# A Mamba block and a mixture of experts on one core: a product moved from VectorE to GpSimd, the gate-up product one slot later, rank matmuls merged

## The reference

```python
x = x + mamba(layernorm(x))     # D_INNER 512, D_STATE 16, D_CONV 4
x = x + moe(layernorm(x))       # 8 experts, top 2, hidden 352, and a shared expert
# in mamba, over the tokens of a sequence:
dA = exp(clip(dt[:, :, None] * A, -5, 5))
state = dA * state + dt[:, :, None] * B[:, None, :] * u[:, :, None] + 1e-06
y = sum(state * C[:, None, :], axis=-1) + D * u
# in moe:
combine = top-2 softmax weights, 0 elsewhere          # tokens x experts
out = sum_e combine[e] * (silu(x @ wg[e]) * (x @ wu[e])) @ wd[e]
out = out + sigmoid(x @ sgw) * (silu(x @ sg) * (x @ su)) @ sd    # shared expert
```

## Time and profile before

| | us |
|---|---|
| median of 3 runs | 2950.19 (2948.59 to 2950.59) |
| the profiled execution, its own time | 2948.53 |
| its span, first to last instruction | 2946.7 |
| busy: PE / PEld / DVE / ACT / POOL | 2601.8 / 2291.2 / 2246.7 / 2030.5 / 2235.6 |
| mean granted TensorE clock | 0.923 of full |

### The profile page before, as it was taken

One profiled execution on the slowest core, in us unless ns is written; L12 is line 12 of the kernel. 1 busy time (PEld: TensorE's weight loads), 2 busy tenths in 40 slices (PEclk: granted clock), 3 DMA queues, 4 the chain that ended last, 5 costly groups with the idle time before them and its releaser, 6 DMA issues.

```text
span 2946.7 us, 49244 instructions
## 1 busy us (share of the span) xinstructions
PE 2601.8 (88%) x15616; PEld 2291.2 (78%) x15616; DVE 2246.7 (76%) x4890; ACT 2030.5 (69%) x4675; POOL 2235.6 (76%) x1354
## 2 busy tenths in 40 slices
PE   7888888888888888888888888888887599999998
PEld 4777877878787778877877778787776488888887
DVE  2989999999998999899989989998998233333332
ACT  3878888888888888888888888888875133333332
POOL 2989998989898989889998989898986033333333
PEclk9889999999999989999999999899987699999999
DMA  4222222222222222222222222222221288888886
GB/s 171 83 77 76 77 77 83 77 76 86 92 83 80 78 84 85 77 88 79 77 76 82 79 76 82 94 85 80 73 81 35 95 199 202 201 202 201 202 200 152
DMA packets 138184, 309.67 MB, mean 105 GB/s; under 512 B 15040, under 2 KB 79680, under 8 KB 137792
## 3 DMA queue, kind: packets, MB, share of 16 engines
q1 hardware_dynamic: 110848, 270.03, 29.5%
q0 software_dynamic: 27072, 36.46, 6.2%
HBM read 258.42 MB, written 48.01 MB: 104 GB/s over the span
## 4 chain that ended last, share of the span: by engine, by line
PE 52%; DVE 22%; ACT 10%; issue 8%; POOL 2%; DMA 1%; SPq 0%; DVEq 0%; ACTq 0%; POOLq 0%
PE bank L662 13%; DVE bank L1242 10%; PE bank L680 9%; PE bank L563 7%; PE bank L600 6%; DVE room L1242 4%; PE bank L552 4%; DVE room L1251 4%; ACT bank L809 3%; ACT room L793 3%; PE bank L530 2%; PE bank L580 2%; PE bank L616 2%; PE bank L570 2%; PE bank L644 2%
## 5 line engine op out<-in xcount | busy, mean ns | idle before, releaser
L1031 POOL TENSOR_TENSOR room<-dtu,b_all 128x1024 f32<-128x1024 f32 x512 | 1202.6, 2370 | 26.4 <-DVE dtu L1419 13.5
L809 ACT ACTIVATE bank<-room,eps_col 128x512 f32<-128x512 f32 x1024 | 693.9, 683 | 282.6 <-DVE carry L1256 202.4
L793 ACT ACTIVATE room<-room,neg_a 128x256 f32<-128x256 f32 x2048 | 867.9, 497 | 0.8 <-DVE room L1208 0.8
L600 PE MATMUL bank<-ident,room 128*128 128x128 f32 x4096 | 589.8, 295 | 236.8 <-DVE room L1251 215.7
L600 PEld LDWEIGHTS bank<-ident,room 128*128 128x128 f32 x4096 | 513.1, 153 | 302.1 <-DVE room L1251 232.3
L1020 POOL TENSOR_TENSOR room<-room,c_all 128x1024 f32<-128x1024 f32 x224 | 532.1, 2375 | 122.9 <-DVE bank L1242 87.7
L1242 DVE TENSOR_TENSOR_SCAN bank<-room,carry,bank 128x256 f32<-128x256 f32 x864 | 580.5, 735 | 48.6 <-ACT bank L809 47.7
L1156 POOL DMA_INDIRECT out<-room,ids x144 | 223.8, 1554 | 409.8 <-DMA out<-room,ids 217.9
L1321 DVE SCALAR_TENSOR_TENSOR hid<-hid,bank 128x256 f32<-128x256 f32 (+1 forms) x312 | 131.1, 420 | 453.8 <-ACT hid L904 453.7
L1242 DVE TENSOR_TENSOR_SCAN room<-room,carry,bank 128x256 f32<-128x256 f32 x672 | 446.1, 728 | 1.1 <-DVE hot L1292 0.5
L552 PE MATMUL bank<-xnT,w_conv 128*128 128x256 f32 x3072 | 404.2, 288 | 7.0 <-ACT xnT L832 5.5
(11 more groups left out here) (150 smaller groups left out, 3095.4 us busy)
## 6 DMA issues: line engine op xcount, KB each, us to landing
b_all<-b_scratch SPq DMA_DIRECT2D x128, 512.0 KB, 4.0
c_all<-b_scratch SPq DMA_DIRECT2D x128, 512.0 KB, 5.5
room<-in_wgu SPq DMA_DIRECT2D x72, 704.0 KB, 5.9
room<-in_wd SPq DMA_DIRECT2D x72, 384.0 KB, 3.6
room<-x_by_expert SPq DMA_DIRECT2D x72, 260.0 KB, 2.9
x_in<-in_x SPq DMA_DIRECT2D x32, 256.0 KB, 6.1
x<-in_x SPq DMA_DIRECT2D x32, 256.0 KB, 2.7
out<-x SPq DMA_DIRECT2D x32, 256.0 KB, 4.2
```

The source lines that it names most:

```text
L600: last = mm(tr_bank[k][:, b * P:(b + 1) * P], v[n % VRING][:, b, k * P:(k + 1) * P], ident[:, :], is_transpose=True, start=False, stop=(n ...
L793: last = af(da[n % RING][:, b, :], dt[c.par][:, b, :], ACT.Exp, scale=neg_a[:, b, n:n + 1])
L809: af(v_slot(c, n, h)[:, :], v[n % VRING][:, 2 * h:2 * h + 2, :].rearrange("p b t -> p (b t)"), ACT.Identity, bias=eps_col[:, 0:1]).then_in ...
L1031: nc.gpsimd.tensor_tensor(out=v[n % VRING][:, :, :], in0=dtu[:, :, :], in1=row, op=ALU.mult) \
```

## The change

Three edits. `BY_POOL` gets a 14: the product C(14) is made by POOL, in its slot 15, in place of DVE; with it go the two small copies on DVE, and ACT gets one `keep_last` more in three chunks of four. `GU_SLOT` and `GATE_SLOT` move unit 2 by one slot on PE and ACT, and a new `GATED_SLOT` moves DVE's multiplies of all three units one slot later. `post_rank` makes the same sums in 7 wider matmuls in place of 13.

```diff
-BY_POOL = [0, 2, 4, 6, 8, 10, 12]
+BY_POOL = [0, 2, 4, 6, 8, 10, 12, 14]
...
-GU_SLOT, GATE_SLOT = [11, 12, 13], [12, 13, 14]
+GU_SLOT, GATE_SLOT, GATED_SLOT = [11, 12, 14], [12, 13, 15], [13, 14, 15]
...
-                for k in range(NT + 1):
-                    place = o_bank[:, k * EXPERTS:(k + 1) * EXPERTS]
-                    mm(place, ones[0:1, :], base[0:1, :], start=True, stop=False)
-                    for b in range(min(k + 1, NT)):
-                        for n in range(PICKS):
-                            last = mm(place, (upper if b == k else ones)[:, :], hot[:, n, b, :], start=False,
-                                      stop=(b == min(k, NT - 1) and n == PICKS - 1))
+                mm(o_bank[:, 0:(NT + 1) * EXPERTS], ones[0:1, :],
+                   base[0:1, :].unsqueeze(1).to_broadcast([1, NT + 1, EXPERTS]), start=True, stop=False,
+                   skip_group_check=True)
+                for n in range(PICKS):
+                    mm(o_bank[:, 0:NT * EXPERTS], upper[:, :], hot[:, n, :, :], start=False, stop=False,
+                       skip_group_check=True)
+                for n in range(PICKS):
+                    for b in range(NT):
+                        later = NT - b
+                        last = mm(o_bank[:, (b + 1) * EXPERTS:(NT + 1) * EXPERTS], ones[:, :],
+                                  hot[:, n, b, :].unsqueeze(1).to_broadcast([P, later, EXPERTS]), start=False,
+                                  stop=(n == PICKS - 1 and b == NT - 1), skip_group_check=True)
...
-                            for u in units_of(slot, GATE_SLOT):
+                            for u in units_of(slot, GATED_SLOT):
                                 gated(post, u, False)
```

## The result

| | before | after |
|---|---|---|
| median, us | 2949.2 (2946.9 to 2951.8, 11 runs) | 2956.8 (2952.2 to 2959.6, 11 runs) |
| ratio after to before, 95% interval | | 1.0024 [1.0015, 1.0033] |
| profiled execution: own time, span, us | 2948.5, 2946.7 | 2952.2, 2950.5 |
| busy, us: PE / DVE / POOL | 2601.8 / 2246.7 / 2235.6 | 2557.6 / 2200.5 / 2308.5 |
| mean granted TensorE clock | 0.923 | 0.934 |

The change makes the kernel 0.24% slower, 7.6 us by the medians. The profiled execution of after happens to be the shortest of its eleven, so the two traces differ by only 3.8 us.

What follows compares the result with a forecast made beforehand. Chains through several engines, with PE waiting for DVE and POOL's queue behind, were taken as the bound. Beat +15, start +2.4 and ends -8 gave +9 us on 2948.5, 2958; with 1.7 for the median, 2959 us, range 2944 to 2977.

Steps and rivals of the forecast that it cites:

- What bounds: In each chunk no engine full; chains through engines set the time: PE waits 202.7 us for DVE, POOL's queue runs behind.
- DVE: In each chunk DVE loses product 14 and two stalls before the gate, so product 15 is ready 3.0 us earlier.
- POOL, +2.35 us in front of `second_weight`: One more C in POOL's queue, placed in front of `second_weight`, costs 2.35 us a chunk.
- T(14) to the convolution, 5.95 to 6.95 us: On PE, T(14), T(15) and the down product up to the convolution, partly at half clock, take 5.95 to 6.95 us.
- The beat: C(2) to C(2) per chunk: mean 69.65 us against 69.14, +0.5 us in each of 29 intervals, +15 us.
- The start: In the first chunk C(14) falls amid POOL's four B's, which have no room: +2.4 us.
- The end, -8: Last scan chunk: DVE keeps its 3.0 us, a 1.91 us stall goes; last routing: fewer rank matmuls, -2.8; together -8 us.
- Edits at nothing: In all other chunks the rank merge, moved gate-up of unit 2, ACT's extra copy and SyncE's order change nothing.
- DVE was the bound: DVE sets the chunk's time, gain at most 3.0 us a chunk: 2858 us, half of it 2900; chance 0.12.
- Half clock throughout: PE at half clock from T(14) to the convolution, 8.3 us: +2.5 us a chunk, about 3020 us; chance 0.13.
- Nothing in the beat: C(2) to C(8) tightens by 0.5 us as ACT gets its banks earlier, beat unchanged: 2945 us; chance 0.15.

Runs made afterwards that it cites:

- e8: The changed kernel with the 13 rank matmuls of before in place of the merged ones; 2966.7 us, ratio 1.0061 to before.
- e3: The kernel of before with only the gate's slots moved, no product moved and no rank merge; 2893.3 us, ratio 0.9806.
- e2: The kernel of before with only the 14 added to `BY_POOL`, one line changed; 2968.1 us, ratio 1.0068.
- e5: The changed kernel with C(14) one instruction earlier in POOL's queue, in front of B(3); 3015.3 us, ratio 1.0220 to before.
- e1: The changed kernel with C(14) put back on DVE, keeping gate slots and merged rank matmuls; 2906.9 us, ratio 0.9859 to before.
- e6: The changed kernel with C(9) on POOL as the eighth product in place of C(14); 2990.7 us, ratio 1.0137 to before.
- e9: The changed kernel with gate-up of unit 2 computed three times, filling PE's pause before T(14); 2986.5 us, ratio 1.0119 to before.

## Why the prediction was right

2959 was forecast, 9 us above a before of 2950.2 (three runs); 2956.8 was measured, 7.6 above 2949.2 (eleven). That these agree within 2 us is in part luck: in the profiled executions, from which the sum was made up, 9.4 us were forecast and 3.8 measured, and the profiled execution of after is the shortest of its eleven. By the steps:

- **What bounds.** Right. The prediction read a chain of PE's waits for DVE, with POOL's queue close behind it. It did not say that the queue was already the bound in one chunk of four of before: the loop of the third chunk of each sequence took 67.50 us, and the C(2) at its end waited for nothing, while the other loops took 68.5 to 70.6. The loop that the prediction adds up, from 1046.32, is one of those that took 67.50.
- **DVE.** Right. Its stalls before the gate are gone, it waits for PE at `post_gate` (L1267, 70.9 us in 30 pieces), and product 15 ends 2.2 us ahead of C(14); 2.3 were forecast.
- **POOL, +2.35 us in front of `second_weight`.** Measured 28.24 - 25.95 = 2.29.
- **T(14) to the convolution, 5.95 to 6.95 us.** In 29 chunks the convolution starts 5.83 to 6.93 us after `second_weight`, 5.74 to 6.83 after T(14). Right, by a partly wrong way: PE was to wait 5 to 6 us for T(14), about once a chunk. It waits twice a chunk (60 waits, 212.1 us), once for C(12), since POOL is late there too. Behind that wait come gate-up of unit 2 and T(13), so that the pause before T(14) is 2.87 us in the chunk shown and 2.8 to 5.8 in the 29. Each pause has a slow stretch behind it: in the chunk shown the granted clock is 0.54 from 1100.1 to 1106.7, 0.99 in the pause before T(14), and 0.71 from T(14) to the convolution. That the way came out as forecast although the pause before T(14) is mostly shorter than forecast is luck.
- **The beat.** 69.65 forecast, 69.59 measured, +13 us over 29 intervals for the +15. From C(2) to C(2), by position in the sequence the loops are 70.17, 70.00 and 69.78 (forecast 69.9), and 68.49 (68.9).
- **The start.** C(14) among the four B's: +2.4 forecast, and the C behind them starts 2.4 us later; by C(2) of the third chunk 1.5 are left.
- **The end, -8.** By the ends of the down products the last scan chunk gave back 5.5 us (5 forecast). The wait for the rank matmuls in the last routing fell from 5.97 to 3.04 us, 2.9 for the 2.8, and some 3 us more went in pieces around it, which were not traced. Sum in the traces: 1.5 + 13.8 - 11.5 = +3.8, where 9.4 were forecast; by the medians +7.6.
- **Edits at nothing.** The merged rank matmuls were put at nothing in every chunk but the last. That was wrong: e8 against after shows 10 us, with a beat of 69.90 against 69.61, 8 us over 28 chunks. So the sum lacks some 8 us of gain in the loop, and its loop of 69.9 us, which has no term for the merge, came close to the changed kernel's 69.98 (the sum of after's pieces) and not to e8's 70.29. Why the merge acts in the loop stays open, as said above.

The last routing's row in after, answering to the earlier trace rows:

```profile
2306.63 0.26 DVE L1310 TENSOR_TENSOR picked<-bank,hot 128x16 f32<-128x16 f32 x2 [3.04 <-PE bank L648]
```

The rivals. *DVE was the bound* falls for the product and holds for the slots: e3 shows that DVE's chain was worth 56 us, to be had without moving a product, and e2 that the product alone loses. The rule of the Trainium skill (Perfetto Trace Analysis, Identifying the Most-Contended Engine) names DVE at 92.1%; relieving it by moving work to the engine at 90.8% made that one the bound (e2, +19 us), and relieving its chain without moving work gained (e3, -56 us). *Half clock throughout*, from T(14) to the convolution, did not come: 5.74 to 6.83 us and not 8.3. The half clock that costs is at another place, which no rival named, behind `proj_bc`: 1 chunk of 21 in after, all 21 in e5, which makes C(14) sooner. *Nothing in the beat* falls by 0.5 us a chunk.

What the prediction did not see is that its own rank and slot edits alone were a gain of 42 us (e1), and the slots by themselves one of 56, since it priced everything with the eighth product in place.

e3 is the best version found: 1.95% below before and 2.15% below the changed kernel.

## What to carry to other kernels

Work out the floor of each engine's queue, the loop time that it would give if it waited only for the one chain that it must, before you move work to it: here 67.5 us for POOL against 69.1 us of beat, a slack of 1.6 us, less than the 2.3 us that the product costs. Run each part of a combined change alone: two gains and a loss, -56, -8 and +19, came out as +8. And when an engine off the critical path is made earlier, look at where it waits next, and whether what it does after that wait gets slower.

## What the runs showed of the hardware

- Making TensorE earlier made the program longer. In e5, e6 and e9 TensorE came to the same wait earlier, and all three took longer than the changed kernel (3015.3, 2990.7 and 2986.5 us against 2956.8); the 21 waits of e5 (4.4 to 5.9 us) were all followed by the 1.2 GHz level, which made the B and C product 3.62 us long in place of 1.91 and C(8) about 2.4 us late in the mean (14.64 against 12.26). The Trainium skill (TensorE: Matmul & The Clock Gate, Why this matters for your kernels) advises against pauses between bursts of matmuls; the traces agree, and add that a pause can come from finishing early.
- The mean granted clock is no measure of progress: e9 has 0.952 and after 0.934, and e9 is 30 us slower.
- POOL's stretches were the same in all kernels to 0.1 us: 15.0 us from `second_weight` to C(2) where it didn't wait, and 25.9 to 26.0 or 28.2 to 28.3 us from C(8), by the number of its products.
